# Two attention and feed-forward layers with a routed expert layer: experts that finish and scatter their own rows, one program for each engine, root steps in PSUM and a new order of the tail's steps

## The chip, the cores and the metric

The kernel runs on one core of one Trainium2 chip. The metric is the device time of one execution in microseconds (us), the median of several executions. The engines are TensorE (PE: matmuls, with PEld for its weight loads), VectorE (DVE), ScalarE (ACT), GpSimd (POOL) and SyncE (SP, which here only issues DMAs). A queue name such as SPq stands for an engine's sequencer that issues a DMA.

## The reference

Input x is 2048 tokens of 128 features. Four sub-layers follow each other, each as x = layernorm(x + f(x)):

1. causal attention with 16 heads of 64 (q, k, v, softmax, output projection);
2. a feed-forward layer of 512 hidden features with weights quantised to -1, 0, 1;
3. an attention with quantised weights and activations; for data whose attention weights all round to zero its output is the projection's bias alone, and a check at run time decides whether that holds;
4. an expert layer. Each token goes to the one of 16 experts with the highest score, and takes a place there if fewer than 128 tokens came before it:

```
score = softmax(xf @ Wg + bg); gate = max(score); idx = argmax(score)
pos   = running number of the token within its expert;  keep = pos < cap   # cap = 128
y     = relu(buf @ W1[e] + b1[e]) @ W2[e] + b2[e]       # buf: the kept rows, by expert and place
out   = where(keep, y[idx, pos] * gate, 0)
x     = layernorm(x + out)
```

A token that finds no place keeps its own row: its result is layernorm(x).

## The kernel before, in words

The kernel is written engine by engine, with semaphores between them, in three programs (`nc.Block`) that run one after the other: `attention`, `attention1_general` and `experts`. Every block ends on all engines before the next begins.

**attention.** The first attention is cut into 320 units (a head, a group of 512 queries, a pair of 128-key tiles). For a unit PE makes scores (L762 to L765), ACT two exponents of it (L1032, L1035), POOL the low half of the float (L1479, `prob_lo = prob - prob_hi`), and PE weighs the values (L788 to L792). At the end of a head and group DVE divides (`invert` L1206, `normalise` L1215, L1219).

From unit 288 on, the *tail* is mixed in: the steps of the other sub-layers for four groups of 512 tokens (g0 to g3). Each engine walks through step numbers i; at number i it does its part of unit i and then the tail steps that the tables `PE_AT`, `ACT_AT`, `DVE_AT`, `POOL_AT` and `ONCE_AT` put there. The numbers are no times, only the order within an engine. For a group the steps are: `project` (PE L826 to L829, 96 matmuls), `norm.0` (DVE: L1284, then `statistics`), the scaling on ACT (L1077), `turn` (PE L840), `x1t` in two halves (ACT L1052, DVE L1293), four `up` (PE L849 to L855, ACT L1061, DVE L1300), four `down` (PE L873, L874), `norm.1` with `third` (DVE: L1284, `statistics`, L1308, `statistics`), `second` (POOL L1486), `third` (ACT L1077), `turn3` (PE L890, ACT L1083), `gate` (PE L898, `choose` on DVE), `count` (PE L573, L576, `slots` on DVE) and `scatter` (POOL L596: four indirect DMAs that put the rows in `expert_rows` in DRAM). `turn.1` and `span` (PE L884, DVE L1319, L1320) and `check` (DVE L1346 to L1370) make the run-time decision of sub-layer 3.

`statistics` calls `one_over_deviation` (L523 to L529): two small operations, twice a reciprocal, a product and a step, then a reciprocal; all of its 128 x 4 operands are in SBUF. Until unit 319 has been weighed the tail has two PSUM banks (4 and 5) for PE's results; a fill waits until the one before it in its bank was given up, which for `project` and `down` is done by the first instruction of `norm` (L1284).

**attention1_general** holds the whole third sub-layer behind an `If` that is not taken for these inputs.

**experts.** SP waits for all scatters and loads the rows back (L1911). PE turns them (L1964); then for each of 16 experts `up` (PE L1974), relu (ACT L1949), `down` (PE L1983), the bias (DVE L2006) and an indirect DMA from POOL that scatters 128 results to `expert_out` in DRAM (L1934). When all 16 have landed, SP loads them back in token order (L1920), DVE multiplies by the gate and adds x (L2011), takes statistics (L2015, L2018, `one_over_deviation`), ACT and DVE scale (L1955, L2025) and SP stores (L1925). The exponent for the gate is ACT L1943.

Of the kernel before, what the change touches and what calls it, by code (L numbers as in the profile page):

```python
# [14 lines left out]
F32 = mybir.dt.float32  # L15
F16 = mybir.dt.float16
BF16 = mybir.dt.bfloat16
I32 = mybir.dt.int32
# [36 lines left out]
ROW = D + 1  # L55
YE = 4
# [179 lines left out]
class Fill:  # L236


    def __init__(self, bank, turn):
# [6 lines left out]
ACT_STAGES = (("norm", 0), ("turn", 0), ("up", 0), ("up", 1), ("up", 2), ("up", 3), ("third", 0), ("turn3", 0), ("turn", 1))  # L246
DVE_STAGES = (("norm", 0), ("turn_low", 0), ("up", 0), ("up", 1), ("up", 2), ("up", 3), ("norm", 1),
              ("gate", 0), ("count", 0), ("span", 0))
POOL_STAGES = (("second", 0), ("scatter", 0))
PE_AT = ((292, 294, 296, 298, 299, 301, 302, 303, 304, 304, 305, 305, 318, 318, 322, 353, 353), (297, 300, 301, 306, 308, 308, 310, 311, 312, 312, 313, 313, 323, 328, 330, 343, 355), (307, 314, 317, 319, 321, 322, 323, 324, 325, 325, 326, 328, 333, 339, 349, 343, 354), (328, 329, 329, 329, 335, 336, 336, 338, 336, 338, 341, 341, 372, 374, 384, 373, 379))  # L250
ACT_AT = ((298, 299, 300, 302, 303, 305, 313, 319, 351), (306, 307, 309, 310, 311, 312, 325, 328, 347), (321, 323, 325, 326, 329, 330, 332, 339, 352), (331, 332, 334, 337, 341, 344, 355, 366, 386))
DVE_AT = ((290, 297, 299, 300, 303, 304, 307, 317, 324, 353), (301, 307, 307, 308, 309, 310, 311, 330, 338, 356), (316, 317, 320, 323, 326, 326, 332, 342, 352, 364), (332, 333, 333, 334, 340, 340, 342, 376, 396, 379))
POOL_AT = ((313, 369), (332, 390), (368, 408), (386, 414))
ONCE_AT = (289, 288, 292, 290, 296, 298, 308, 320, 329, 333, 359, 360, 288, 396)
# [135 lines left out]
class Tail:  # L390


    def __init__(self, nc, m, kept):
# [25 lines left out]
        self.gate = keep("gate", [P, TILES])  # L419
# [8 lines left out]
        self.work = [keep(f"work{i}", [P, TILES]) for i in range(3)]  # L428
        self.root = keep("root", [P, 2, TILES])
# [7 lines left out]
        self.ex = at("ex", w + 8192, [P, TILES, EXPERTS])  # L437
        self.stats16 = at("stats16", w + 9216, [P, TILES, 6])
        self.mv16 = at("mv16", w + 9600, [P, TILES, 2])
        self.rstd16 = at("rstd16", w + 9728, [P, TILES])  # L440
        self.shift16 = at("shift16", w + 9792, [P, TILES])
# [34 lines left out]
        self.xet = at("xet", m.PROB + 8256, [P, EXPERTS * CAP])  # L476
        self.b1r = at("b1r", m.PROB + 16448, [EXPERTS, FF])
        self.h = [at(f"h{i}", m.PROB + 18496 + 2048 * i, [P, FT, CAP]) for i in range(2)]
        self.ye = [at(f"ye{i}", m.PROB + 22592 + 512 * i, [P, D]) for i in range(YE)]
        self.er = at("e_r", m.HIGH[1], [P, TILES, D])  # L480
        self.back = at("back", m.KQ, [P, TILES, D])
# [5 lines left out]
        self.rows_out = nc.dram_tensor("expert_out", (S, D), F32, kind="Internal").ap()  # L487

    def sems(self, sem):
# [17 lines left out]
        self.ext_ready, self.asked, self.expd = sem("ext_ready"), sem("asked"), sem("expd")  # L507
# [11 lines left out]
def one_over_deviation(dve, c, t, out, variance, n=4):  # L519

    half, s, q = (work[:, 0:n] for work in t.work)
    half_eps, bits = (t.root[:, k, 0:n] for k in range(2))
# [9 lines left out]
def statistics(dve, c, t, x, n, g, off_ready=None):  # L532

    s = slice(4 * g, 4 * g + 4)
    for k in range(4):
        c.mark(dve.bn_stats(t.stats[:, k, :], x[:, k, :]))
# [4 lines left out]
    one_over_deviation(dve, c, t, t.rstd[:, n, s], t.mv[:, n, s, 1])  # L541
    last = dve.scalar_tensor_tensor(t.off[:, n, s], t.mv[:, n, s, 0], -1.0, t.rstd[:, n, s], ALU.mult, ALU.mult)
# [50 lines left out]

def scatter(pool, t, k):
# [4 lines left out]

def clear_rows(queue, t):  # L600
# [3 lines left out]
    queue.dma_start(t.rows_out.rearrange("(e c) d -> c e d", c=P), wide[:, :, 0:D]).then_inc(t.filled, 16)  # L604


def attention(nc, m, t, ins, sem):
# [46 lines left out]
    with nc.Block() as block:  # L654

        @block.tensor
        def _(pe):
            def take(what):
                if what.turns > 0:
                    pe.wait_ge(free[what.buf], what.turns)  # L660
                if what.after is not None:
                    pe.wait_ge(ride_placed, what.after.ride + 1)
                return m.buf[what.buf]

            def turn_x(job):
                b = job.group
                pe.wait_ge(x_loaded[b], 16)
                if b > 1:
                    pe.wait_ge(xt_low, b - 1)
                for t in range(4):  # L670
                    last = pe.transpose(m.psum[:, 6 + b % 2, t * P:(t + 1) * P], m.x[b // 2][:, 4 * (b % 2) + t, :], m.ident[:])
                last.then_inc(x_turned, 1)

            def kq(job):
                out = take(job)
                if job.pair == 0:
                    pe.wait_ge(xt_low, job.group + 1)
                    pe.wait_ge(w_low, 1)
                elif job.pair == 1:
                    pe.wait_ge(w_low, 4)  # L680
                c = slice(job.group * 512, (job.group + 1) * 512)
                w = slice(job.pair * P, (job.pair + 1) * P)
                for k in range(2):
                    o = out[:, k * 512:(k + 1) * 512]
                    pe.matmul(o, m.w_hi[:, k, w], m.xt_hi[:, c], start=True, stop=False)
                    pe.matmul(o, m.w_hi[:, k, w], m.xt_lo[:, c], start=False, stop=False)
                    last = pe.matmul(o, m.w_lo[:, k, w], m.xt_hi[:, c], start=False, stop=True)  # L687
                last.then_inc(full[job.buf], 1)

            def values(job):  # L690
                out = take(job)
                if job.pair == 0:
                    pe.wait_ge(xt_low, 2 * job.group + 2)
                    pe.wait_ge(w_low, 2)
                w = slice(job.pair * P, (job.pair + 1) * P)
                for t in range(8):
                    tok = slice((8 * job.group + t) * P, (8 * job.group + t + 1) * P)
                    o = out[:, t * P:(t + 1) * P]
                    pe.matmul(o, m.xt_hi[:, tok], m.w_hi[:, 2, w], start=True, stop=False)
                    pe.matmul(o, m.xt_hi[:, tok], m.w_lo[:, 2, w], start=False, stop=False)  # L700
                    last = pe.matmul(o, m.xt_lo[:, tok], m.w_hi[:, 2, w], start=False, stop=True)
# [1364 lines left out]
```

## Time and profile before

| what | value |
|---|---|
| median of three runs | 926.57 us (924.73 to 926.93) |
| profiled execution, own time | 924.85 us |
| its span | 923.0 us |
| PE, DVE, ACT, POOL busy | 790.1, 614.6, 634.3, 641.9 us |
| mean granted TensorE clock | 0.937 |
| attention's last weighing ends | about 788.8 us |
| last scatter of rows issued by POOL | 852.1 us |
| experts' rows loaded from | 860.1 us |
| last `down` ends | about 898.5 us |

The span runs from the program's first instruction to its last. A clock of 1.00 is 2.4 GHz and 0.50 is 1.2 GHz. Starts of instructions are in us from the start of the span, durations in us or, where marked mean, in ns.

### The profile page before, as it was taken

The numbers are of one execution on the slowest core, as the hardware profiler recorded it, in microseconds if no ns is written. First come the engines' busy times: TensorE is split into PE (matmuls) and PEld (weight loads), VectorE is DVE, ScalarE is ACT, GpSimd is POOL, SyncE is SP. The second block draws the span as 40 slices with busy tenths as digits, with TensorE's granted clock in tenths as the row PEclk, the third lists the DMA queues.
The fourth block names the chain that finished last, engine by engine and source line by source line (L and its number), as shares of the span: only waits on it lengthen the run. The fifth ranks groups of instructions, "written<-read, shape, count | busy, mean of one in ns | idle before, by whom it ended". The sixth has DMA issues, their size and how long they took to land. (4 is left out here: it accounts for less than half of the span.)

```text
span 923.0 us, 25964 instructions
## 1 busy us (share of the span) xinstructions
PE 790.1 (86%) x10829; PEld 516.5 (56%) x10829; DVE 614.6 (67%) x1338; ACT 634.3 (69%) x855; POOL 641.9 (70%) x401
## 2 busy tenths in 40 slices
PE   6778999989999999999999999999989975774590
PEld 3344555556666656665666566666657644542590
DVE  5697777677766767667766667766674749858015
ACT  4356777878888788888888888888876753231351
POOL 5356767878888888798878888898886736116050
PEclk9799999999999999999999999999999977856695
DMA  5222136141214122312322141214320100700353
GB/s 164 59 47 48 30 87 131 31 99 25 48 27 90 25 48 65 64 25 53 71 42 42 37 99 24 48 39 91 98 31 19 14 2 1 224 30 21 82 180 93
DMA packets 91087, 56.59 MB, mean 61 GB/s; under 512 B 39876, under 2 KB 87368, under 8 KB 90838
## 3 DMA queue, kind: packets, MB, share of 16 engines
q1 hardware_dynamic: 89222, 51.87, 24.9%
q8 instruction: 87, 1.43, 0.7%
q0 software_dynamic: 1024, 1.45, 0.5%
q10 hardware_dynamic: 720, 1.57, 0.5%
q14 instruction: 34, 0.28, 0.1%
HBM read 16.51 MB, written 5.26 MB: 24 GB/s over the span
## 5 line engine op out<-in xcount | busy, mean ns | idle before, releaser
L1479 POOL TENSOR_TENSOR prob_lo<-prob,prob_hi 128x1024 f16<-128x1024 f32 (+1 forms) x320 | 583.2, 1842 | 165.2 <-ACT prob L1035 127.0
L1171 DVE TENSOR_REDUCE part_max<-psum 128x2 f32<-128x1024 f32 (+1 forms) x320 | 333.3, 1059 | 87.4 <-PE psum L717 66.5
L1032 ACT ACTIVATE prob_hi<-psum 128x1024 f16<-128x1024 f32 (+1 forms) x320 | 288.5, 902 | 135.4 <-PE psum L765 131.2
L1035 ACT ACTIVATE prob<-psum 128x1024 f32<-128x1024 f32 (+1 forms) x320 | 288.5, 902 | 0.0
L762 PE MATMUL psum<-high 128*128 128x512 f16 (+3 forms) x640 | 225.4, 352 | 29.4 <-DVE part_max L1171 11.2
L788 PE MATMUL psum<-v,prob_hi 128*128 128x65 f16 x2176 | 235.0, 194 | 0.3 <-issue 0.2
L790 PE MATMUL psum<-v,prob_hi 128*128 128x64 f16 x2176 | 233.1, 193 | 0.0
L792 PE MATMUL psum<-v,prob_lo 128*128 128x65 f16 x2176 | 233.1, 195 | 0.0
L788 PEld LDWEIGHTS psum<-v,prob_hi 128*128 128x128 f16 x2176 | 201.0, 98 | 36.6 <-issue 17.1
L765 PE MATMUL psum<-mixed 65*128 65x512 f16 (+3 forms) x640 | 221.4, 351 | 0.0
L790 PEld LDWEIGHTS psum<-v,prob_hi 128*128 128x128 f16 x2176 | 202.0, 98 | 14.4 <-issue 0.6
L792 PEld LDWEIGHTS psum<-v,prob_lo 128*128 128x128 f16 x2176 | 201.6, 97 | 0.0
L717 PE MATMUL psum<-kq 64*128 64x512 f16 (+3 forms) x640 | 113.7, 358 | 13.6 <-DVE part_max L1171 5.1
L762 PEld LDWEIGHTS psum<-high 128*128 128x128 f16 x640 | 62.9, 98 | 88.9 <-issue 21.3
L1153 DVE TENSOR_TENSOR kq<-psum,kq 128x1024 f16<-128x1024 f32 x32 | 39.2, 1225 | 67.2 <-ACT kq L1002 67.2
L765 PEld LDWEIGHTS psum<-mixed 65*128 65x128 f16 x640 | 62.5, 98 | 36.8 <-issue 1.1
L717 PEld LDWEIGHTS psum<-kq 64*128 64x128 f16 x640 | 30.9, 93 | 68.3 <-DVE part_max L1171 23.4
L764 PE MATMUL psum<-mask_ki,corner 128*128 128x128 bf16 x256 | 56.0, 219 | 0.0
L1219 DVE SCALAR_TENSOR_TENSOR turned<-psum,inv_sum,turned 128x64 f16<-128x64 f32 x224 | 48.1, 278 | 2.0
L1162 DVE TENSOR_TENSOR v<-psum,v 128x512 f16<-128x512 f32 x32 | 20.6, 686 | 36.9 <-ACT v L1014 36.9
L1486 POOL TENSOR_SCALAR x<-r,mv,rstd 128x128 f32<-128x128 f32 x16 | 12.5, 794 | 45.1 <-DVE x L1308 45.1
L1002 ACT ACTIVATE kq<-psum 128x1024 f16<-128x1024 f32 x32 | 33.0, 1031 | 11.7 <-PE psum L687 11.1
(213 smaller groups left out, 920.4 us busy)
## 6 DMA issues: line engine op xcount, KB each, us to landing
high<-kq SPq DMA_DIRECT2D x128, 128.0 KB
mixed<-kq SPq DMA_DIRECT2D x64, 128.0 KB
ew<-in_L_ffn_W SPq DMA_DIRECT2D x32, 256.0 KB, 5.1
expert_rows<-zero SPq DMA_DIRECT2D x1, 1032.0 KB, 8.3
xe<-expert_rows SPq DMA_DIRECT2D x4, 258.0 KB, 4.1
prob<-in_L_attn_x SPq DMA_DIRECT2D x4, 256.0 KB, 5.9
mixed<-shift SPq DMA_DIRECT2D x64, 1.0 KB
expert_out<-zero SPq DMA_DIRECT2D x1, 1024.0 KB, 11.1
```

What stands on the lines that cost most here:

```text
L717: last = pe.matmul(o, m.kq_hi[rows, 1, q], m.kq_hi[rows, 0, k], start=(n == 0), stop=(c < g), skip_group_check=True)
L762: pe.matmul(o, k_hh[:, keys], q_hl[:, queries], start=True, stop=False)
L764: pe.matmul(o[:, 0:P], m.identb, m.mask_ki[:], start=False, stop=False)
L765: last = pe.matmul(o, k_l1[:, keys], q_hm[:, queries], start=False, stop=True)
L788: pe.matmul(acc[:, r, 0:HD + 1], hi[:, c], v[:, j, HD:VW], start=(j == 0 and r == 0), stop=False, skip_group_check=True)
L790: pe.matmul(acc[:, r, 0:HD], hi[:, c], v[:, j, 0:HD], start=False, stop=False, skip_group_check=True)
L792: last = pe.matmul(acc[:, r, 0:HD + 1], lo[:, c], v[:, j, HD:VW], start=False, stop=end, skip_group_check=True)
L1032: act.activation(m.prob_hi[i % HI_RING][:, 0:u.width], src, ACT.Exp, scale=EXP_SCALE)
L1035: act.activation(m.prob[i % PROB_RING][:, 0:u.width], src, ACT.Exp, scale=EXP_SCALE)\
L1171: last = dve.tensor_reduce(m.part_max[:, g % 2, :, r, c:c + 1], src[:, :, col:col + width], AX, ALU.max)
L1219: last = dve.scalar_tensor_tensor(lo[:, r, :], acc[:, r, 0:HD], inv[:, r:r + 1], hi[:, r, :], ALU.mult, ALU.subtract)
L1479: pool.tensor_tensor(m.prob_lo[i % LOW_RING][:, c], m.prob[i % PROB_RING][:, c], m.prob_hi[i % HI_RING][:, c], ALU.subtract).then_inc(low, 1)
```

## The change

- Each row that is scattered to an expert carries, besides its token's number, the share `1 / sum(exp)` (`ROW` 130 instead of 129). ACT makes the exponents by group (`ex`), DVE the share (`share`), both as new tail steps ahead of the scatter.
- The experts' DVE program first makes layernorm(x3) of all 2048 rows and SP stores them to the output (1 MB). For each expert DVE then forms gate * b2 + x (`spread`), adds gate * y (`add`), takes statistics, ACT takes a square root (`Sqrt`), DVE divides, and POOL scatters the finished rows over the output. The buffers `ye` are 7 instead of 4. The gathering back, the passes over 16 tiles and the last store are gone.
- The three programs are one: SP fetches the experts' rows as soon as the scatters have landed; the decision of sub-layer 3 is waited for on a semaphore (`judged`), and each engine reads it for itself.
- In `statistics` the operands `half`, `s` and the reciprocal for the offset are in the PSUM bank of the sum, so that no step reads two SBUF operands. One reciprocal is added, and the bank is given up at the end of the statistics and not after L1284.
- All tables of the tail's order are new. Among other moves PE's `project` of g2 (307, 314, 317) is at 315 and 316; DVE's `gate` of g1 goes behind `norm.0` of g3, and `gate` of g2 ahead of g3's `up`; DVE's `spread` goes ahead of `norm.1` of g2; ACT's `third` of g2 goes ahead of `norm.0` of g3; POOL's `scatter` of g0 goes ahead of `second` of g2.
- `clear_rows` clears one DRAM tensor and not two.

```diff
-ROW = D + 1
-YE = 4
+ROW = D + 2
+YE = 7
...
-PE_AT = ((292, 294, 296, 298, 299, 301, 302, 303, 304, 304, 305, 305, 318, 318, 322, 353, 353), (297, 300, 301, 306, 308, 308, 310, 311, 312, 312, 313, 313, 323, 328, 330, 343, 355), (307, 314, 317, 319, 321, 322, 323, 324, 325, 325, 326, 328, 333, 339, 349, 343, 354), (328, 329, 329, 329, 335, 336, 336, 338, 336, 338, 341, 341, 372, 374, 384, 373, 379))
+PE_AT = ((292, 292, 293, 298, 299, 300, 303, 304, 305, 305, 305, 306, 318, 318, 321, 372, 380), (297, 299, 300, 306, 309, 310, 311, 312, 312, 313, 313, 314, 326, 336, 341, 346, 373), (315, 316, 316, 318, 319, 322, 323, 326, 325, 330, 331, 332, 337, 338, 371, 373, 391), (333, 333, 333, 337, 344, 345, 348, 350, 351, 356, 357, 367, 404, 405, 424, 384, 415))
+ACT_AT = ((299, 299, 299, 301, 305, 306, 317, 323, 383, 326), (307, 310, 310, 311, 312, 314, 324, 334, 385, 365), (324, 324, 324, 327, 327, 329, 331, 336, 387, 374), (334, 336, 340, 342, 359, 364, 389, 402, 412, 423))
+DVE_AT = ((291, 293, 294, 295, 295, 304, 305, 316, 317, 373, 323), (294, 306, 306, 306, 309, 314, 314, 340, 370, 392, 366), (314, 316, 316, 320, 320, 325, 329, 353, 383, 415, 383), (334, 340, 354, 355, 357, 366, 372, 408, 433, 423, 431))
+POOL_AT = ((308, 364), (317, 464), (416, 483), (435, 490))
...
-    c.step(dve.scalar_tensor_tensor(half, variance, 0.5, half_eps, ALU.mult, ALU.add))
+    c.step(dve.tensor_scalar(half, variance, 0.5, 0.5 * EPS, ALU.mult, ALU.add))
...
-    c.step(dve.reciprocal(out, s))
+    c.mark(dve.reciprocal(out, s))
...
+    half, root, over = place[:, 0:4], place[:, 16:20], place[:, 32:36]
...
+    one_over_deviation(dve, c, t, t.rstd[:, n, s], t.mv[:, n, s, 1], half, root, t.work[:])
+    c.step(dve.reciprocal(over, root))
+    last = dve.scalar_tensor_tensor(t.off[:, n, s], t.mv[:, n, s, 0], -1.0, over, ALU.mult, ALU.mult)
...
+        c.step(dve.tensor_tensor(t.r[g][:], bank(fill).rearrange("p (a n) -> p a n", n=D), x, ALU.add))
+        statistics(dve, c, t, t.r[g], n, g, bank(fill), None if n else t.off_ready)
+        if n == 0:
+            give_up(fill, g, 0)
...
+        pool.wait_ge(t.shared, g + 1)
...
+    def sync(sp):
+        sp.wait_ge(t.scattered, 16 * TILES)
+        fetch(sp, t)
+        sp.wait_ge(t.judged, 1)
+        taken = sp.value_load(t.bad[0:1, 0:1], min_val=0, max_val=1)
...
+    def gpsimd(pool):
+        pool.wait_ge(plain_stored, 16 * GROUPS)
+        for e in range(EXPERTS):
+            if e % 4 == 0:
+                pool.wait_ge(t.xe_in[e // 4], 16)
+            pool.wait_ge(y_ready, e + 1)
+            pool.indirect_dma_start(rows_out, bass.IndirectOffsetOnAxis(xe[:, e, D:D + 1].bitcast(U32), 0),
...
+    def scalar(act):
+        act.wait_ge(t.zeroed, 7)
+        act.activation(t.spare[:], t.eps[:], ACT.Sqrt)
+        act.wait_ge(plain_var, 1)
+        act.activation(t.std16[:], t.mv16[:, :, 1], ACT.Sqrt, bias=t.eps[:]).then_inc(plain_root, 1)
...
+        def root(e):
+            act.wait_ge(row_var, e + 1)
+            act.activation(t.std_e[:, e:e + 1], t.mv_e[:, e, 1:2], ACT.Sqrt, bias=t.eps[:]).then_inc(row_root, 1)
...
+            last.then_inc(up_done, 1)
+            if e > 1:
+                root(e - 2)
+        root(EXPERTS - 2)
+        root(EXPERTS - 1)
...
+        def spread(e):
...
+            c.step(dve.scalar_tensor_tensor(ye[e % YE][:], t.eb2[:, e, :], xe[:, e, D + 1:D + 2], xe[:, e, 0:D],
+                                            ALU.mult, ALU.add))
+
+        def add(e):
+            y = ye[e % YE][:]
+            dve.wait_ge(down_full, e + 1)
+            dve.scalar_tensor_tensor(y, m.psum[:, 6 + e % 2, 0:D], xe[:, e, D + 1:D + 2], y, ALU.mult, ALU.add)\
+                .then_inc(down_done, 1)
+            dve.wait_ge(down_done, e + 1)
+            c.step(dve.bn_stats(t.stats_e[:, e % 2, :], y))
+            dve.bn_aggr(t.mv_e[:, e, :], t.stats_e[:, e % 2, :]).then_inc(row_var, 1)
+
+        def normal_rows(e):
+            y = ye[e % YE][:]
+            dve.wait_ge(row_root, e + 1)
+            c.step(dve.reciprocal(t.rstd_e[:, e:e + 1], t.std_e[:, e:e + 1]))
+            dve.tensor_scalar(y, y, t.mv_e[:, e, 0:1], t.rstd_e[:, e:e + 1], ALU.subtract, ALU.mult).then_inc(y_ready, 1)
...
+        for e in range(EXPERTS):
+            if e < EXPERTS - 1:
+                spread(e + 1)
+            add(e)
+            if e > 0:
+                normal_rows(e - 1)
+        normal_rows(EXPERTS - 1)
```

## Rows read from the trace of the kernel before

**Rows 1.** Busy time by stretch: PE, PEld, DVE, ACT, POOL, clock, DMA share, GB/s.

```profile
736.00:747.00 11.00, 3.11 (x17) 0.82 (x13) 8.02 (x31) 1.86 (x3) 2.12 (x1) 0.73 0.00 0
...
770.00:781.00 11.00, 0.69 (x23) 0.57 (x19) 10.34 (x32) 0.53 (x2) 7.66 (x7) 0.73 0.00 0
781.00:789.00 8.00, 7.15 (x74) 6.46 (x74) 5.58 (x37) 4.00 (x10) 0.00 (x0) 0.51 0.01 3
...
814.00:828.00 14.00, 13.84 (x65) 7.93 (x64) 7.43 (x33) 3.47 (x6) 0.00 (x0) 0.50 0.01 1
```

**Rows 2.** Timeline of DVE at two places: start, us, instruction, idle before.

```profile
731.40 2.10 DVE L527 TENSOR_TENSOR work<-work 128x4 f32<-128x4 f32 x1
...
733.95 1.87 DVE L527 TENSOR_TENSOR work<-work 128x4 f32<-128x4 f32 x1
...
760.55 0.69 DVE L1284 TENSOR_TENSOR r<-psum,x 128x512 f32<-128x512 f32 x1 [3.54 <-PE psum L874]
```

**Rows 3.** Groups of DVE's instructions, 728 to 782 us: busy, mean ns, idle.

```profile
L527 DVE TENSOR_TENSOR work<-work 128x4 f32<-128x4 f32 x8 | 8.8, 1097 | 0.3
L528 DVE SCALAR_TENSOR_TENSOR work<-work 128x4 f32<-128x4 f32 x8 | 5.1, 636 | 0.3
L1308 DVE SCALAR_TENSOR_TENSOR x<-r,rstd,pb_b 128x128 f32<-128x128 f32 x8 | 4.7, 645 | 0.1
...
L542 DVE SCALAR_TENSOR_TENSOR off<-mv,rstd 128x4 f32<-128x4 f32 x4 | 2.1, 520 | 0.1
```

**Rows 4.** One of the same groups, 796 to 836 us.

```profile
L528 DVE SCALAR_TENSOR_TENSOR work<-work 128x4 f32<-128x4 f32 x10 | 1.6, 162 | 0.3
```

**Rows 5.** Timeline of POOL at its last units, and a PSUM-reading group of DVE.

```profile
763.42 11.11 POOL L1479 TENSOR_TENSOR prob_lo<-prob,prob_hi 128x1024 f16<-128x1024 f32 x6
...
L1219 DVE SCALAR_TENSOR_TENSOR turned<-psum,inv_sum,turned 128x64 f16<-128x64 f32 x224 | 48.1, 278 | 2.0
```

**Rows 6.** Timeline of PE: the two long waits of the attention.

```profile
743.56 0.58 PE L849 MATMUL psum<-onesb,bias 3*128 3x512 bf16 x1 [6.48 <-DVE x1t L1293]
...
781.16 1.09 PE L890 MATMUL psum<-ident,x 128*128 128x128 f32 x4 [10.47 <-DVE r L1284]
```

**Rows 7.** Timeline, 784 to 863 us: ACT, DVE, POOL and SP.

```profile
784.38 1.65 ACT L1077 ACTIVATE x<-r,off,rstd 128x128 f32<-128x128 f32 x4 [1.50 <-DVE off L542]
...
797.51 0.68 DVE L1284 TENSOR_TENSOR r<-psum,x 128x512 f32<-128x512 f32 x1
...
831.97 3.15 POOL L1486 TENSOR_SCALAR x<-r,mv,rstd 128x128 f32<-128x128 f32 x4 [19.99 <-DVE x L1308]
...
852.10 0.98 POOL L596 DMA_INDIRECT expert_rows<-x,slotu  x1 [0.30 <-issue]
...
860.10 2.85 SPq L1911 DMA_DIRECT2D xe<-expert_rows  x4
```

**Rows 8.** DMA of the rows' scatter, from issue to landing, 800 to 870 us.

```profile
DMA to landing us min/median/max: 2.1/2.4/4.5
```

**Rows 9.** Groups of the experts' stage, 870 to 897 us.

```profile
L1949 ACT ACTIVATE h<-psum,b 128x128 f32<-128x128 f32 x64 | 18.2, 368 | 10.2 <-PE psum L1974 10.2
...
L2006 DVE TENSOR_TENSOR ye<-psum,eb 128x128 f32<-128x128 f32 x14 | 4.1, 292 | 21.6 <-PE psum L1983 21.6
```

**Rows 10.** Timeline from the last `down` to the end.

```profile
898.54 0.29 DVE L2006 TENSOR_TENSOR ye<-psum,eb 128x128 f32<-128x128 f32 x1 [1.20 <-PE psum L1983]
899.61 0.97 POOL L1934 DMA_INDIRECT expert_out<-ye,xe  x1 [0.53 <-issue]
901.83 2.02 SPq L1920 DMA_DIRECT2D back<-expert_out  x4
...
906.00 0.87 DVE L2015 BATCH_NORM_STATS2 stats<-e_r 128x6 f32<-128x128 f32 x4
```

**Rows 11.** Timeline of ACT: its one table load, and its smallest exponent.

```profile
3.27 1.28 ACT L1124 ACT_TABLE_LOAD   x1 [3.27 <-issue]
...
850.77 0.21 ACT L1116 ACTIVATE small<-small 1x16 f32<-1x16 f32 x1 [11.05 <-DVE small L1360]
```

More of the change, by code:

```diff
@@ L255 @@
+ONCE_AT = (288, 289, 290, 289, 294, 296, 316, 322, 329, 326, 359, 379, 309, 434)
 WIDE = ()
@@ L427, in __init__ @@
         self.off = keep("off", [P, 3, TILES])
-        self.work = [keep(f"work{i}", [P, TILES]) for i in range(3)]
-        self.root = keep("root", [P, 2, TILES])
+        self.work = keep("work", [P, 4])
+        self.root = keep("root", [P, 4])
         self.x = at("x", m.XT, [P, TILES, D])
@@ L591, in slots, with exponents_of, share @@
     dve.tensor_copy(t.slotu[:, s], t.slot[:]).then_inc(t.slots_ready, 1)
+def exponents_of(act, t, g):
+    s = slice(4 * g, 4 * g + 4)
+    act.activation(t.ex[:, s, :], t.lm[:, s, :], ACT.Exp).then_inc(t.ex_ready, 1)
+def share(dve, c, t, g):
+    c.step(dve.tensor_reduce(t.total[:], t.ex[:, 4 * g:4 * g + 4, :], AX, ALU.add))
+    dve.reciprocal(t.x3[g][:, :, D + 1], t.total[:]).then_inc(t.shared, 1)
 def scatter(pool, t, k):
@@ new lines, in scale, with place_third @@
+        def scale(g, n):
+            act.wait_ge(t.off_ready, OFFS.index((g, n)) + 1)
+            for k in range(4):
+                j = 4 * g + k
+                x = t.x3[g][:, k, 0:D] if n else t.x1[g][:, k, :]
+                last = act.activation(x, x if n else t.r[g][:, k, :], ACT.Identity, scale=t.rstd[:, n, j:j + 1],
+                                      bias=t.off[:, n, j:j + 1])
+            last.then_inc(t.x3_ready[g] if n else t.x1_ready[g], 1)
+        def place_third(g):
+            fill = wait_full(act, "turn3", g)
+            act.activation(t.x3t[g][:], bank(fill), ACT.Copy).then_inc(t.tail_free[fill.bank], 1)
@@ new lines, in third @@
+        def third(g):
+            x = t.x3[g][:, :, 0:D]
+            dve.wait_ge(t.early, 16 * 3)
+            for k in range(4):
+                last = dve.scalar_tensor_tensor(x[:, k, :], t.r[g][:, k, :], t.rstd[:, 1, 4 * g + k:4 * g + k + 1],
+                                                t.pb_b[:], ALU.mult, ALU.add)
+                if k < 3:
+                    c.mark(last)
+            last.then_inc(t.mean_ready, 1)
+            c.wait()
+            dve.wait_ge(t.mean_ready, g + 1)
+            fill = FILLS["down", g, 0]
+            statistics(dve, c, t, x, 2, g, bank(fill), t.off_ready)
+            give_up(fill, g, 2)
@@ new lines, in spread_rows @@
+        def spread_rows():
+            dve.wait_ge(t.row_in, 16 * 13)
+            c.mark(dve.reciprocal(t.prm[:, 0:2, :], t.row[:, QA:QA + 2, :]))
+            c.step(dve.tensor_scalar(t.prm[:, 2:4, :], t.row[:, QZ:QZ + 2, :], ROUND, -ROUND, ALU.add, ALU.add))
+            for n, src in enumerate((t.row[:, BQ:BQ + 2, :], t.prm[:, 0:2, :], t.prm[:, 2:4, :], t.row[:, QA:QA + 2, :])):
+                dst = t.spread[:, n, :].rearrange("a (b h d) -> a b h d", b=2, d=H1)
+                c.mark(dve.tensor_copy(dst, src.unsqueeze(3).broadcast_to([1, 2, HEADS, H1])))
+            c.wait()
@@ new lines, in vector @@
+        dve.memset(m.mixed[0][HD:HD + 1, 1, :], 1.0).then_inc(ones, 1)
+        run(PLAN[-1])
+        for i in range(NU):
+            if i > 1 and UNITS[i - 2].last:
+                invert(UNITS[i - 2])
+            run(PLAN[2 * i])
+            if i + 2 < NU and UNITS[i + 2].rider is not None:
+                place_shift(UNITS[i + 2].rider)
+            run(PLAN[2 * i + 1])
+            if i > 1 and UNITS[i - 2].last:
+                normalise(UNITS[i - 2])
+            tail(i)
+        invert(UNITS[NU - 1])
@@ L1878, in _ @@
[L1878 to L1884 removed]
+                    pe.wait_ge(dve_done, d0 + 10)
+                    for k in range(TILES):
+                        last = pe.transpose(flat(4)[:, k * P:(k + 1) * P], e[:, k * P:(k + 1) * P], m.ident[:])
```

2344 lines of the change are left out of this document (1148 added, 1196 removed).

## The prediction

> **What bounds the kernel now.** I began with busy time by stretch, because the page's shares are averages. In most of the 788 us of attention PE is full, but it did 3.11 us of work in the 11 us from 736 and 0.69 us in the 11 us from 770, and ran at 1.2 GHz for the 8 us behind that [rows 1]. PE's timeline names who ended those two waits: DVE both times, after 6.48 and 10.47 us [rows 6]. So I read DVE's timeline there. Four-element-wide products that take 0.16 us elsewhere took 2.10 and 1.87 us [rows 2, 4]. Grouped over 54 us, the products average 1097 ns, the steps 636 and the offset 520, where a quiet stretch has 162 for such a step [rows 3, 4]. At that time POOL ran its prob_lo subtractions end to end, 1.85 us each, and DVE's operations with one input in PSUM keep 278 ns all through the attention [rows 5]. The reader is to see that only operations with both inputs in SBUF stretch, and to about the length of a POOL instruction.
>
> Behind the attention one chain of small steps runs to the scatter. POOL sets its last part: from 831.97 it does second (3.15 us), then twelve scatters back to back, the last issued at 852.10 [rows 7]. Then nothing works until SP's fetch at 860.10, though a scatter lands in 2.4 us [rows 7, 8]. In the experts PE is full: 27 us hold 15 experts' worth, 1.79 us each, while ACT's four relus and DVE's bias wait for it [rows 9]. The last bias is at 898.54, its scatter at 899.61, the load back at 901.83, and the passes and the store run to 923.0 [rows 10].
>
> **The change, part by part**, against the profiled execution (span 923.0, own time 924.85).
>
> *Root steps in PSUM.* The long waits removed are 8 x (1.097 - 0.162) for the products, 8 x (0.636 - 0.162) for the steps and 4 x (0.520 - 0.162) for the offset: 7.5 + 3.8 + 1.4 = 12.7 us [rows 3, 4]. Of these 3.6 us lie in the first place (2.10 + 1.87 - 2 x 0.162) [rows 2], the rest, 9.0, in the second, and both chains are the ones PE waits for [rows 6]. L1308 has two SBUF inputs and stays as slow as it is (645 ns). What PSUM costs a small operation no row shows directly; L1219 has it at 278 ns for 64 elements, a step without it takes 162 for 4 [rows 4, 5]. I take 0 and, as the upper bound, 0.1 us for each of eight steps. The added reciprocal is one more small step with its wait: 0.2 us a statistics call. The Trainium skill, "SBUF — State Buffer" (section on the two sides), says that a VectorE operation with two SBUF inputs and a GpSimd operation that reads SBUF exclude each other for the whole instruction; by that rule, which the trace agrees with, L1308 still waits, and no root step does.
>
> *The new order, up to the last unit.* In the first place I walked through both orders with the durations of the rows. Sums and project of g0 are earlier, so norm.1 of g0 begins some 1.4 us earlier; PE's up of g1 (now at step 309, was 308) is ready 5.0 us earlier (3.6 + 1.4) and still finds DVE busy, since norm.1 and third last 11 us. Project of g2 moved behind down of g1 takes 48 matmuls, about 2.9 us, off the way to down. So norm.1 of g1, at 760.55 [rows 2], begins at about 752.6: 7.9 us earlier. From there to the scaling of g2 at 784.38 [rows 7] are 23.8 us. Less 9.0 of waits, less 1.4 for the division of unit 311 that now comes before it, plus three reciprocals (0.6), that is 14.0. The bank is now held until the statistics end, 3.5 us more for a project and 8.7 for a down. PE needs 11 us for the units and project up to step 318, so here it waits 2 to 3 us in place of 10.47, and that is all of the holds that I find exposed. ACT, which now scales third of g1 first, starts g2's scaling 0.6 late. Gain so far: 7.9 + 9.8 - 0.6 = 17.1 us.
>
> *The order behind the attention.* g2's last up now waits in PSUM bank 7 for the division of unit 319, which DVE does behind count of g0: 1.6 us late. The gate of g1 no longer stands before norm.1 of g2 (797.51 [rows 7], 2.0 us of DVE, of which 1.6 counted). The row parameters' spread, 1.3 us, now does. Four statistics calls add 0.8, and PE's gate and turn before g3's up take about what gate of g2 gives back. Net a loss of 2.1. So POOL's second of g3, at 831.97, starts 15.0 us earlier. From there POOL is the bound as before, 20.1 us to the last issue; DVE's slots of g3, with share and a span more, are ready within 0.5 us of POOL's need for them.
>
> *One program.* SP fetches when the scatters have landed, 852.10 + 2.4 = 854.5 in old time, not at 860.10: 5.6 us gained [rows 7, 8]. What hides behind the fetch (3 us to the first rows): the check, 6.5 us of DVE, ends before the last scatter is issued; each engine's reading of the decision, unpriced in the trace, costs between 0 and the 5.6 us of the old gap. The pass over 16 tiles comes behind it on DVE: 16 statistics at 0.22 and 16 aggregates, 5 us [rows 10], on which ACT's first square root waits, and behind that the evacuation of the turned rows. PE turns all four batches first, which gives it just under 1 us to spare; I take 0, the bound is 4. The store of 1 MB comes after the fetch on SP and ahead of the first result's scatter, some 8 us later.
>
> *The experts.* A 128x128 operation of DVE takes 0.29 [rows 9]; per expert there are now spread 0.29, add 0.29, statistics 0.22, aggregate 0.1, reciprocal 0.18 and normalise 0.25: 1.5 us with waits, under PE's 1.79. ACT has 4 x 0.284 = 1.14 and a root of one column, 0.21 by the smallest exponent [rows 9, 11]: 1.4. Both hide behind PE; without that cover, the excess over 1.79 is paid 16 times.
>
> *The end.* From 898.54: add 0.3, statistics and aggregate 0.4, the root of expert 15 beside normalise of 14, then normalise of 15: its row is ready at 900.3. POOL takes expert 14 at about 900.5 and needs 0.97 + 0.30 for each, so 15 goes at 901.8 and lands 2.15 later, as the old one did (899.61 to 901.76) [rows 10]: 904.0. Against 923.0 that is 19.0 gained.
>
> Sum: 17.1 - 2.1 + 5.6 + 19.0 = 39.6 us. Span 883.4, own time 885.3; the three runs' median is 1.7 above the profiled execution, so 887.
>
> **The rivals.** (a) *The banks held longer bite.* Only two banks serve the tail under the attention, and five fills before unit 319 are held 3.5 or 8.7 us longer, 27.9 in all. If half of that is exposed on PE, 14 us of the first gain go: 901. For it: DVE serves these steps in order, behind norms of 4 and 9 us. Against it: the fills of a group follow some units apart. (b) *PE keeps its clock.* With shorter waits the 14 us at 1.2 GHz from 814 and the 8 us from 781 [rows 1] may run at 2.4: up to half of the 22 us less, 876. For it: in these rows the clock is low in and behind stretches in which PE idled. Against it: the chain of g3 still idles PE. (c) *DVE becomes the experts' bound.* At 2.1 us instead of 1.5 it costs 16 x 0.3 = 5, 892. For it: six dependent operations with semaphores. (d) *ACT loads its table anew for every root and back.* One load, 1.28 us, served Copy, Exp, Identity and Relu for the whole run [rows 11]; Sqrt is new. If each root takes two loads and each drains an activation of 0.3 us first, ACT needs 1.4 + 2 x 1.6 = 4.6 us an expert, 2.8 over PE, 45 us in all, and the kernel is slower: 932. It decides from 1.79 + 39.6 / 16 = 4.3 us on. Against it: Copy, Relu and Exp already share a load. The Trainium skill, "ScalarE: Activation LUTs" (table sets), puts Sqrt in a set other than Exp's but Relu and Copy in every set; by that, one more load, hidden. The same page prices a switch at 2.66 us; two of those an expert would give about 966, an estimate.
>
> **How the numbers follow.** Forecast as summed 0.50, (a) 0.22, (b) 0.13, (c) 0.10, (d) 0.05. The range 874 to 902 takes in (a) to (c) and, around the forecast, PSUM's upper bound (some 4 us), the decision's reading (4 us) and the fetch. Of the forecast's cases none is slower. About 0.3% is what a measurement of this kernel can tell from no change. Faster 0.94, same 0.01, slower 0.05.
>
> **What would show it.** After: L527, L528 and L542's successors under 0.25 us beside POOL's subtractions, L1308's still at 0.3 to 0.7; PE's longest waits near 5 and 3 us; the fetch 2 to 3 us behind the last scatter's issue; experts at 1.79 us each and one further table load; last `down` to the end 5.5 us. The forecast is wrong if PE waits for banks 4 and 5 before unit 319 (a), if an expert takes over 1.9 us (c, d), or if PE waits for ACT or DVE after the rows have landed.

## The result and the profile after

The changed kernel took 892.65 us (889.11 to 896.50, four runs) against 926.17 for the kernel before on the same chip: ratio 0.9641, interval 0.9597 to 0.9684, 3.6% faster. I had forecast 887, in a range of 874 to 902. The profiled execution is the fastest of the four: span 887.3, own time 889.11, so its gain is 35.7 us of the 39.6 that I had summed.

Busy time by stretch, the stretches that answer to [rows 1], with some others of the same table left out:

```profile
736.00:747.00 11.00, 8.32 (x82) 4.27 (x83) 3.59 (x13) 4.09 (x7) 6.62 (x6) 0.69 0.00 1
...
770.00:781.00 11.00, 10.62 (x86) 5.93 (x83) 6.60 (x30) 2.75 (x6) 0.00 (x0) 0.50 0.15 28
...
797.00:814.00 17.00, 15.65 (x94) 9.36 (x94) 9.84 (x52) 5.96 (x14) 0.00 (x0) 0.57 0.03 8
```

PE now has work in the two stretches in which it had next to none: 8.32 us of 11 where it had 3.11, 10.62 of 11 where it had 0.69. But the second runs at 1.2 GHz (0.50) in its whole length, and so does most of 797 to 814: the clock that was low behind the waits is low in other stretches now, in which PE works. The small steps of DVE, grouped over 700 to 800 us (the columns are busy time and mean ns of one), answer to [rows 3] and [rows 4]:

```profile
L528 DVE RECIPROCAL work<-psum 128x4 f32<-128x4 f32 x19 | 3.5, 182 | 0.6
L1334 DVE SCALAR_TENSOR_TENSOR x<-r,rstd,pb_b 128x128 f32<-128x128 f32 x12 | 3.4, 349 | 0.1
...
L530 DVE SCALAR_TENSOR_TENSOR psum<-psum,work 128x4 f32<-128x4 f32 x20 | 3.4, 170 | 0.7
L529 DVE TENSOR_TENSOR work<-work,psum 128x4 f32<-128x4 f32 x20 | 3.1, 157 | 0.7
```

157 to 182 ns each (the offset, L547, 158). What took 1097 and 636 in the mean is gone, and PSUM costs a small step nothing. L1334 is the old L1308, with two inputs in SBUF: 349 ns here, where I had said that it stays at 645. What PE waited for up to 822, with the total, the number of waits and the longest (its two long ones of before, in the attention, were 6.48 and 10.47 [rows 6], and a third of 10.05, for ACT's scaling, stood behind it at 811.88):

```profile
PE psum L870 <- DVE x1t L1319: 5.3, 3, 4.5
PE psum L919 <- ACT x3t L1103: 4.8, 1, 4.8
PE psum L861 <- POOL x L1516: 4.2, 1, 4.2
...
PE psum L919 <- DVEq L1313: 2.0, 1, 2.0
```

The longest is 4.8 us, and only the 2.0 us for DVEq, DVE's late release of a bank, belong to the holds. The third wait listed is new: PE turns the rows that POOL's second makes, and stands behind it. The two ends of the part that I had put figures on are ACT's scaling of g2, at 767.41 for 784.38 [rows 7] (17.0 us earlier; I had 17.1), and POOL's second of g3 with the last scatter's issue:

```profile
767.41 1.63 ACT L1097 ACTIVATE x<-r,off,rstd 128x128 f32<-128x128 f32 x4
...
818.33 3.12 POOL L1516 TENSOR_SCALAR x<-r,mv,rstd 128x128 f32<-128x128 f32 x4 [25.59 <-DVE x L1334]
...
837.92 0.97 POOL L613 DMA_INDIRECT expert_rows<-x,slotu  x1 [0.30 <-issue]
```

818.33 for 831.97 is 13.6 us (I had 15.0), and from there POOL needs 19.6 us, as before 20.1. Then the timeline from the end of the check to the first expert:

```profile
839.50 0.14 DVE L1398 TENSOR_SCALAR bad<-small 1x1 int32<-1x1 f32 x1
840.04 2.04 SPq L621 DMA_DIRECT2D xe<-expert_rows  x4
840.60 1.28 ACT L1989 ACT_TABLE_LOAD   x1 [2.15 <-issue]
...
844.38 3.19 DVE L2076 BATCH_NORM_STATS2 stats<-x 128x6 f32<-128x128 f32 x16 [4.73 <-issue]
...
845.58 3.65 PE L2019 MATMUL psum<-ident,xe 128*128 128x128 f32 x16 [13.17 <-issue]
...
849.65 2.05 PE L2029 MATMUL psum<-xet,ew 128*128 128x128 f32 x16 [0.42 <-ACT xet L1994]
```

The fetch is at 840.04, 20.1 us earlier than [rows 7] has it. But the first rows have landed by 843.1, and PE turns them only at 845.58. The flag itself is late as well: the check ends at 839.64, 1.7 us behind the last scatter's issue, where I had it ahead of it, and all engines but SP read it from 839.68 on. The chain of waits says who was the last there:

```profile
840.66 3.71 issue
844.38 3.20 DVE stats L2076 x16
...
848.80 0.31 ACT std L1991
849.11 1.95 ACT xet L1994 x4
```

"issue" for 3.71 us is DVE, idle behind the flag that it wrote itself at 839.50. The trace's record of branch instructions shows what it does there: all five engines load the flag in 0.47 to 0.55 us, and then PE's branch over the general path takes 4.48 us (840.54 to 845.02); DVE's own branch takes 0.07, but its first instruction behind it begins 3.7 us later. ACT's, over a short path, takes 0.05. From DVE the chain goes on through the pass over the plain rows, ACT's root at 848.80 and ACT's copies, to PE's first up at 849.65. Fetch to first up is 9.6 us; before it was 7.6.

The experts, from the first up to the end of the last down, take 30.3 us (30.8 before). The end, from PE's last down:

```profile
878.76 1.16 PE L2038 MATMUL psum<-ew,h 128*128 128x128 f32 x8 [0.34 <-ACT h L2005]
...
879.96 0.35 DVE L2063 SCALAR_TENSOR_TENSOR ye<-psum,xe,ye 128x128 f32<-128x128 f32 x1
...
880.85 0.97 POOL L1983 DMA_INDIRECT out_x<-ye,xe  x1 [0.85 <-DVE ye L2073]
...
882.12 0.97 POOL L1983 DMA_INDIRECT out_x<-ye,xe  x1 [0.30 <-issue]
883.40 0.97 POOL L1983 DMA_INDIRECT out_x<-ye,xe  x1 [0.30 <-issue]
```

PE ends at 879.92, the last scatter is issued at 883.40 and has landed by 885.5. Last down to the end is 7.4 us; before, it was 24.5 [rows 10]. Step by step the gain of 35.7 is: up to the fetch 20.1, fetch to first up -2.0, the experts 0.5, the end 17.1.

### The profile page after: what moved, and what is told of

The parts are those of the page before. It is cut to its first block, busy times and chain, and to the rows that moved or that the text cites. A ratio compares the mean times of both kernels' runs of the same rounds, so it can differ in the third digit from the quotient of the medians.

```text
span 887.3 us, 26048 instructions
## 1 busy us (share of the span) xinstructions
PE 788.5 (89%) x10829; PEld 512.2 (58%) x10829; DVE 616.7 (70%) x1418; ACT 635.9 (72%) x869; POOL 640.9 (72%) x401
## 4 chain that ended last, share of the span: by engine, by line
PE 60%; DVE 23%; ACT 10%; issue 5%; DMA 1%; POOL 0%; SPq 0%; POOLq 0%; DVEq 0%; ACTq 0%
PE psum L783 12%; PE psum L786 10%; DVE part_max L1193 9%; PE psum L738 7%; PE psum L809 6%; PE psum L813 5%; PE psum L811 5%; ACT prob_hi L1052 3%; DVE kq L1175 3%; ACT prob L1055 3%; ACT kq L1022 2%; DVE turned L1241 2%; PE psum L2038 1%; ACT v L1034 1%; PE psum L2029 1%
## 5 line engine op out<-in xcount | busy, mean ns | idle before, releaser
L1983 POOL DMA_INDIRECT out_x<-ye,xe x16 | 15.5, 970 | 30.0 <-DMA out_x<-e_r 19.2
```

## The experiments

All runs have their own runs of the kernel before beside them (924.9 to 926.5 us). The first four build the change up from the kernel before: the root steps alone, the order alone, both, and both with one program.

**Root steps in PSUM alone.**

```diff
-    half, s, q = (work[:, 0:n] for work in t.work)
+    half, root, over = place[:, 0:4], place[:, 16:20], place[:, 32:36]
...
-    dve.tensor_tensor(t.r[g][:], bank(fill)..., x, ALU.add).then_inc(t.tail_free[fill.bank], 1)
-    wait_free(dve, "down" if n else "project", g)
+    c.step(dve.tensor_tensor(t.r[g][:], bank(fill)..., x, ALU.add))
+    ...
+    give_up(fill, g, 0)
```

> The kernel before with the root steps' operands in PSUM alone (bank kept until the statistics end, the second reciprocal added), its order, its three blocks and its experts as they were. My theory: the stretched steps and products fall to some 0.17 us each, 3.6 us in the first place where PE waits and 9.0 in the second, less 0.8 for four reciprocals and at most 2 for the banks held: 914 to 916 us against 926.2. Rival, the banks held longer bite in this order: over 920, with PE waiting for a bank of the tail. Rival, the steps were short in the changed kernel only because another order keeps them away from POOL's subtractions: they stay at 0.6 to 1.1 us here and the time stays at 926.

It took 936.0 us (932.2 to 944.2), ratio 1.0115 [1.0071, 1.0158]: 10 us slower than before, where my theory had 11 faster. Its steps, in the same kind of view (690 to 800 us), and PE's waits up to 822:

```profile
L1314 DVE SCALAR_TENSOR_TENSOR x<-r,rstd,pb_b 128x128 f32<-128x128 f32 x8 | 10.4, 1362 | 0.1
...
L527 DVE SCALAR_TENSOR_TENSOR psum<-psum,work 128x4 f32<-128x4 f32 x14 | 2.4, 170 | 0.5
```

```profile
PE psum L892 <- DVEq L1293: 10.8, 1, 10.8
PE psum L820 <- DVEq L1293: 9.9, 2, 7.2
PE psum L851 <- DVEq L1293: 3.2, 1, 3.2
```

The steps are as short as in the changed kernel though POOL's subtractions stand beside them as before, so it is PSUM that shortens them, not the order. The old wait of 6.48 us has all but gone (0.6). L892's 10.8 stands in the place of the old wait of 10.47, and the 13.2 us for L820 and L851 are new. PE's timeline has them as three waits of 2.7, 3.2 and 7.2 us, each for a bank that DVE gives up at the end of its statistics. L892 too now waits for such a release (DVEq) and no longer for the sum (L1284), so part of it is a hold as well; a fifth wait of this kind, 4.9 us, comes behind 822, at 847.52. And L1314, the large product with two inputs in SBUF, takes 1362 ns where it took 645, 5.7 us more in all: with the small ones gone, this one meets POOL's subtractions.

**The new order alone**, as a diff the five tables of steps, without the entries for the exponents and the share.

> The kernel before with the new order of steps alone (the steps for the exponents and the share left out of it). My theory: 1.4 us from sums and project of g0, 2.9 from project of g2 behind down of g1, less 2.1 lost behind the attention: 922 to 925 us against 926.2, with root steps that still take 0.6 to 1.1 us beside POOL. Rival, the order is what brought the gain inside the attention: 912 or less.

926.6 us (twelve executions), ratio 1.0005 [0.9989, 1.0021]. The order alone gives nothing. The stretch that PSUM would have taken away now falls on other steps:

```profile
L542 DVE SCALAR_TENSOR_TENSOR off<-mv,rstd 128x4 f32<-128x4 f32 x7 | 7.1, 1020 | 0.2
L523 DVE SCALAR_TENSOR_TENSOR work<-mv,root 128x4 f32<-128x4 f32 x7 | 6.7, 958 | 0.2
```

The offset takes 1020 and the first step 958 ns in the mean, where the product took 1097 before. Moving DVE's work against POOL's changes which step is hit.

**Both.**

> The kernel before with both: root steps in PSUM and the new order; three blocks and the experts as they were. My theory: the gains add up to 15.0 us at POOL's second of g3, so 911 us (909 to 914). If the two overlap (each takes the same wait away) the sum is less than that of the two single runs; if the order only pays once the steps are short, it is more than it.

910.9 us, ratio 0.9856 [0.9825, 0.9888]: 15.4 us faster, as forecast (15.0), though one part alone costs 9.7 and the other gives nothing. The two don't add up: with the short steps the order takes the exposed holds away (one of 2.1 us is left up to 822), and without the short steps it is worth nothing.

**Both and one program for each engine**, with the experts' old end.

> As the run before, and in addition one program for each engine, with the fetch of the rows ahead of the decision; the experts still scatter to the internal tensor, load back, and divide and normalise at the end (no exponents or share ahead of the scatter). My theory: 5.6 us less than with three blocks, 905 to 906. Against the changed kernel it should be some 13 us slower: 17 to 19 for the end, less some 4 to 5 for the pass over the plain rows that the changed kernel has between fetch and first expert. Rival, the block boundaries were hidden behind the scatters' landing: no more than 2 us less than with three blocks.

907.3 us, ratio 0.9797 [0.9768, 0.9825]: 3.5 us less than with three blocks, in place of 5.6, though the two intervals touch. The changed kernel, which differs by the experts' new end and the exponents and shares ahead of the scatter, took 892.7, 14.7 us less (I expected some 13). Its timeline from the last scatter's issue to the first expert:

```profile
842.99 0.97 POOL L611 DMA_INDIRECT expert_rows<-x,slotu  x1 [0.30 <-issue]
...
845.11 2.03 SPq L619 DMA_DIRECT2D xe<-expert_rows  x4
...
850.28 3.64 PE L2012 MATMUL psum<-ident,xe 128*128 128x128 f32 x16 [12.34 <-issue]
...
853.72 2.45 PE L2022 MATMUL psum<-xet,ew 128*128 128x128 f32 x14
```

The fetch is 2.1 us behind the last issue; with three blocks it was 7.8 (838.27 and 846.10). That is 5.7 us, where I had 5.6. But fetch to first up takes 8.6 us where it took 7.1: PE's jump over the general path now lies behind the fetch. The branch records of the kernel before show it at its old place, 3.62 us of PE from 856.11, between two block ends, inside the 8 us ahead of the fetch. Nothing hid it there: PE is the last engine to reach the second block's end, at 859.79, and the fetch follows at 860.10. So more than half of the 5.6 us is this jump, and it was moved, not removed.

**The changed kernel again**, for its spread and as the level for the runs beside it.

> The changed kernel once more, as the level for the three runs beside it: 892.7 us, 889 to 897. The kernel before spread by only some 4 us over 17 executions. If the granted clock of an execution goes with its time here too, the spread is the throttle's; if not, it is a wait that falls now one way and now the other.

893.6 us, ratio 0.9668 [0.9628, 0.9708]. Three executions took 889.3 to 889.9 at a mean granted clock of 0.950 to 0.956, three 897.4 to 898.7 at 0.941 to 0.943.

**The root steps' operands in SBUF again**, all else as changed.

```diff
-    half, root, over = place[:, 0:4], place[:, 16:20], place[:, 32:36]
+    half, root, over = (t.scratch[:, k, :] for k in range(3))
```

> The changed kernel with the three operands of the root steps in SBUF again and all else as it is, the banks still kept until the statistics end. In the three kernels run so far the order without PSUM roots gave 926.6 us and with them 910.9, so I expect what they gave there, some 15.7 us: 908 us (904 to 911). Rival, the new order alone keeps the small steps away from POOL's subtractions: under 897.

918.3 us, ratio 0.9913 [0.9885, 0.9941]. So, with banks that are held this long anyway, the roots' place in PSUM is worth 24.7 us; the rival is out, and my 15.7 was too little. PE's waits say why:

```profile
PE psum L871 <- DVE x1t L1320: 10.9, 3, 10.1
...
PE psum L912 <- DVEq L1314: 3.9, 1, 3.9
PE psum L871 <- DVEq L1314: 3.8, 1, 3.8
PE psum L920 <- DVEq L1314: 3.2, 1, 3.2
PE psum L840 <- DVEq L1314: 2.8, 1, 2.8
```

13.7 us of waits for banks given up late (DVEq) and 10.9 for DVE's low part. Stretched steps inside a held bank stretch the hold too. My 15.7 was from kernels of which the one without PSUM roots held nothing.

One row of this run goes against the reading that only operations with two SBUF inputs stretch:

```profile
L526 DVE TENSOR_SCALAR scratch<-mv 128x4 f32<-128x4 f32 x7 | 7.0, 998 | 0.2
```

This step has one SBUF input and constants, and writes to SBUF; four of its seven took 1.46 to 1.68 us. With its result in PSUM, as in the changed kernel, it takes 166 ns. The reciprocals, with one SBUF input too, stay at 178 ns or less in the mean.

**Old order, PSUM for the banks of down only.**

> The kernel before, old order, with root steps in PSUM for the statistics that use the bank of down (norm.1 and third) and in SBUF for those of the project (norm.0), whose bank is given up behind the sum as before. With all of them in PSUM it took 936.0 us and TensorE waited 13.2 us for banks given up late, in three waits (2.7, 3.2 and 7.2). Theory: the two shorter waits are for banks of a project, the 7.2 for one of a down; so some 6 us less with this one, 930, and still over the kernel before. Rival: the banks of down do no harm and nearly all the loss is the projects': 920 to 924, faster than the kernel before.

928.0 us, ratio 1.0024 [1.0001, 1.0047], 8 us less than with all roots in PSUM. PE's waits:

```profile
PE psum L893 <- DVE r L1287: 7.6, 1, 7.6
PE psum L821 <- DVEq L1298: 7.5, 1, 7.5
```

The two shorter waits are gone and the one of 7.5 us stays, which is the one for the bank of down. In the place of L892's 10.8 us PE waits 7.6 us for the sum, so some 3 of those were a hold too. The large product takes 1407 ns here. So the old order fails by both holds, and it is not faster even without the projects'.

**Without the decision.** The flag is not read and the general path is not there; this part of the computation is left out.

> The changed kernel without the reading of the flag and without the general path that it guards (that part of the computation is left out; the inputs don't need it). In the changed kernel's trace the branch takes TensorE 4.48 us and DVE about as long, and TensorE turns its first rows 2.5 us after they have landed. Theory: that is exposed, and with it the later start of the pass over the plain rows, so 2.5 us faster than the changed kernel, with the first transposes right behind the first landing. Rival: the landing of the rows and the plain pass hide it, same time within 1 us.

Its median, 893.8 us, ratio 0.9639 [0.9606, 0.9673], is that of the changed kernel. But its profiled execution was 4 us late at the very first sum (701.2 for 697.3), in code that is the same in both, and 7.1 at second of g3. This is no effect of the edit: in a later profile of the changed kernel itself (`after_third`) the sum is at 700.6 and second of g3 at 824.8, 6.5 late, and in both of these profiles the clock is at 1.2 GHz from 694 to 697, where it is at 2.4 in the first. What lies behind the fetch can still be compared: PE turns rows 2.9 us behind it in place of 5.5, the first up comes 6.6 us behind it in place of 9.6, and fetch to end takes 43.9 us for 47.3. But here the clock rises 6.3 us behind the fetch, ahead of the first up, and in the changed kernel 9.2 us behind it. So not all of the 3.4 us need be the decision's. The whole does not show it, so the rival is refuted for the piece alone.

**The decision turned round.** Nothing is left out.

```diff
+        with pe.If(taken < 1):
+            rest[0](pe)                 # the experts' part, for every engine
         with pe.If(taken):
             enter(pe)
...
             leave(pe)
+            rest[0](pe)
-                for part in (first, general, last):
+                for part in (first, general):
```

> The changed kernel with the decision turned round: the case that the inputs take falls through into the experts, which stand inside it, and the general path (with the experts once more behind it) lies behind them and is jumped over at the very end. Nothing is left out. Theory: a branch that is not jumped costs TensorE some tenths of a microsecond in place of 4.48, so the gain of the run without the decision less about 0.5: 2 us faster than the changed kernel. Rival: the long time is that of the reading or of any branch, jumped or not, and nothing is gained; the jump at the end could also cost some 4 us on the last engine.

890.2 us, ratio 0.9636 [0.9599, 0.9674].

```profile
840.42 2.03 SPq L621 DMA_DIRECT2D xe<-expert_rows  x4
...
841.06 3.19 DVE L2091 BATCH_NORM_STATS2 stats<-x 128x6 f32<-128x128 f32 x16 [1.04 <-issue]
...
843.44 3.87 PE L2034 MATMUL psum<-ident,xe 128*128 128x128 f32 x16 [10.51 <-DMA xe<-expert_rows]
...
847.10 1.28 PE L2044 MATMUL psum<-xet,ew 128*128 128x128 f32 x5
```

PE's branch takes 0.09 us, DVE begins its pass 1.0 us behind the flag, not 4.7, and PE turns the rows as they land. The first up is 6.7 us behind the fetch, for 9.6. But fetch to end is 46.3 us, only 1.0 less than in the changed kernel. The experts take 31.4 us for 30.3 and the end 8.2 for 7.4. In both kernels the granted clock is 0.56 to 0.58 from 845 to 850 and 1.00 from there: the work that PE takes up earlier it does at 1.2 GHz. The 0.8 us at the end are not the jumps of PE and DVE, which are done by 883.0. The last scatter lands 3.1 us behind its issue, where it took 2.2, and GpSimd's closing drain takes 4.95 us for 4.63; why both are longer is open.

> The kernel whose branch falls through, a second time. Its trace gave 1.0 us less from fetch to end than the changed kernel's, its median 3.4 less, with executions that spread by 10 us. If the gain is the 1.0 us of the trace, the two medians here differ by less than their spread can tell; if they are again over 2 us apart, something ahead of the fetch gained too.

> The changed kernel a third time, as the level for the run beside it: 893 us, 889 to 899.

887.2 us, ratio 0.9585 [0.9559, 0.9612], beside 889.6, ratio 0.9620 [0.9597, 0.9643], for the changed kernel. The two intervals overlap. Fetch to end is 45.8 for 47.0. Over all executions the medians are 888.6 (12) and 891.5 (15). This is the best kernel that I have, by 1.0 to 1.2 us from fetch to end in the two pairs of traces and by 2 to 3 in medians of executions that spread by 10. The medians are again over 2 us apart. The code ahead of the fetch is the same in both, so what could have gained there is the clock: it was 0.950 to 0.962 in the six executions of this kernel and 0.942 to 0.956 in the five of the changed kernel beside them. No run separates the two.

The profiles of the changed kernel also say what its spread is. PE worked at 1.2 GHz for 59.5 us in the first, with a span of 887.3, and for 72.3 us in the third, with 894.5 (its busy time within the stretches of that clock). The 12.8 us more at half speed are 6.4 of the 7.2 us between them.

**The last rows' order**, on top of it.

```diff
         for e in range(EXPERTS):
+            if e == EXPERTS - 1:
+                root(e - 2)
             act.wait_ge(up_full, e + 1)
...
+            if e == EXPERTS - 2:
+                normal_rows(e - 1)
             add(e)
```

> The kernel whose branch falls through into the experts (its profiled span from the fetch to the end was 46.3 us, against 47.3 in the changed kernel), and in addition the last three rows' order: expert 13's root stands before the relus of 15 on ACT, and its normalising before the sum of expert 14 on DVE, so that GpSimd does not get three scatters in a row behind the last matmul. Theory: row 13 leaves 1.3 us earlier, the last relus start 0.3 to 0.6 late, so 0.7 to 1.0 us less from the last rows' matmuls to the end: 45.4 us from fetch to end, 889 us in all where the clock falls as it did in that run. Rival: the last relus' delay takes it all, 46.3.

890.5 us, ratio 0.9615 [0.9588, 0.9641], fetch to end 46.7 us: nothing gained.

```profile
881.53 1.16 PE L2055 MATMUL psum<-ew,h 128*128 128x128 f32 x8 [0.63 <-ACT h L2022]
...
882.23 0.29 ACT L2013 ACTIVATE std_e<-mv_e,eps 128x1 f32<-128x1 f32 x1 [0.75 <-DVE mv_e L2084]
882.72 0.35 DVE L2080 SCALAR_TENSOR_TENSOR ye<-psum,xe,ye 128x128 f32<-128x128 f32 x1 [0.53 <-PE psum L2055]
...
883.70 0.34 DVE L2090 TENSOR_SCALAR ye<-ye,mv_e,rstd_e 128x128 f32<-128x128 f32 x1
...
884.84 0.97 POOL L1998 DMA_INDIRECT out_x<-ye,xe  x1 [1.02 <-DVE ye L2090]
886.11 0.97 POOL L1998 DMA_INDIRECT out_x<-ye,xe  x1 [0.31 <-issue]
```

ACT's last relus start behind root 13, and PE's last down waits 0.63 for them, where it waited 0.34: that much the rival had. The other part I had overlooked. Root 14 is there by 882.52 while DVE is idle, but DVE's order has the sum and the statistics of row 15 first, so row 14 is ready only at 884.04 and the scatters of 14 and 15 still come back to back, the last one 3.42 us behind the last down's end, where it was 3.48. The two rows' order would have to be changed together; that was not tried.

## Why the prediction was right, and where its terms were not

*Root steps.* Right in mechanism and in size: the steps are 0.16 to 0.18 us, and the run with SBUF operands brings the waits back. PSUM itself cost 0, as I had taken. The failed sentence is that L1308 "stays as slow as it is (645 ns)"; my list of signs had allowed 0.3 to 0.7. In the changed kernel it takes 349, in the two with the old order and operands in PSUM 1362 and 1407. What stretches is whichever two-input SBUF operation lies beside POOL's subtractions, so its mean belongs to a schedule and not to the instruction. This is how the Trainium skill, "SBUF — State Buffer" (section on the two sides), puts it, and for two-input operations these traces agree. Too narrow was my "only operations with both inputs in SBUF stretch": a step with one SBUF input took 998 ns in the mean in the run with operands in SBUF.

*The order up to the last unit.* 17.0 us measured for 17.1, but not by the parts that I had. The large product of g0, before and after:

```profile
736.46 2.94 DVE L1308 SCALAR_TENSOR_TENSOR x<-r,rstd,pb_b 128x128 f32<-128x128 f32 x4
...
733.14 1.14 DVE L1334 SCALAR_TENSOR_TENSOR x<-r,rstd,pb_b 128x128 f32<-128x128 f32 x4
```

norm.1 of g0 begins at 728.97 for 728.74, 0.2 us later where I had it 1.4 earlier. PE's up of g1 is 4.9 us earlier all the same (I had 5.0), because this product gave 1.8 us that I had put at nothing. norm.1 of g1 begins at 754.02, 6.5 us earlier for 7.9, and from there to the scaling of g2 the gain is 10.4 us for 9.2. That the sum is right to 0.1 us is luck. I had found only "2 to 3 us" of the holds exposed, and it is 2.0. Rival (a) is nevertheless no idle one: in the old order the same holds cost at least 13.2 us and turn the gain into a loss. I had judged it on the new order, and rightly, but had split the 17.1 into "waits" and "order" as if each could be had alone. The order's own 1.4 and 2.9 us, less the 2.1 behind the attention, don't exist by themselves: alone it gave 0.

*Behind the attention.* A loss of 3.4 where I had 2.1 (13.6 for 15.0 at second of g3). No run tells which of its small terms was short. POOL's 20.1 us were 19.6.

*One program.* The fetch came as forecast, 5.9 us closer to the last issue for 5.6. The step that failed is "I take 0, the bound is 4" for what lies behind it: it cost 2.0 us. Two things together make them: DVE and PE stand 3.7 and 4.5 us in the jump, and the pass over the plain rows, which I had behind the check with PE's work to hide it, starts that much later. I had named the decision "between 0 and the 5.6 us of the old gap" and put it behind the check, where I took the landing to hide it. I also had the check end before the last scatter is issued, and it ended 1.7 us behind it. Had it ended with that issue, PE's jump would have been over at 843.3, about when the first rows landed; that is worked out from the trace, no run tried it. In the run without the decision the piece from fetch to end is 3.4 us shorter, part of it at a higher clock.

*The experts.* 1.79 us each, DVE and ACT under PE, one further table load (1.28 us at 840.60). Rivals (c) and (d) are out.

*The end.* 17.1 for 19.0. The last issue was right (3.5 us behind the last down for 3.3), the landing too (2.1). I had let the kernel end with the landing; the kernel before ends 0.4 us behind the landing of SP's store. The changed kernel, whose last transfers are GpSimd's own, ends 1.8 us behind. The trace's records show GpSimd's closing drain run for 4.6 us and end 1.5 us after SP has seen the last landing.

*The median.* 3.5 above the profiled execution for 1.7, because the changed kernel's executions spread by up to 10 us where those of before spread by 4 to 7. Rival (b): PE's work at 1.2 GHz did not shrink, it moved (770 to 781 now; 797 to 814 at 0.57). All time at 1.2 GHz fell from 117 to 86 us (mean clock 0.937 and 0.952), but PE worked for 56 us of it before and for 60 now, so no gain came from it.

Every large term was right within 2 us. Of the 3.9 us that the sum had too much in the profiled execution, 2.0 lie between the fetch and the first up and 1.9 at the end; 0.5 lost ahead of the fetch and 0.5 gained in the experts cancel.

## What to carry to other kernels

An operand moved into PSUM is free for the instruction and not for the bank: count how long each bank is held and who wants it next, and lay out the order for that, since here the same edit cost 10 us in the old order and gave 16 in the new one (926.6 to 910.9). Before taking a block boundary out, ask what lies inside it and where that goes: here a jump of 3.6 us over a large body moved from ahead of the fetch to behind it. Put the path that the data takes where it falls through; here that gave 1.0 to 1.2 us from fetch to end.

## What the runs showed that I had not expected

- PE's jump over the general path took 3.3 to 4.9 us in every kernel that has it (4.48 here, 3.62 before), ACT's and GpSimd's, over shorter paths, 0.04 to 0.05; not jumped, the same branch took PE 0.09. The length alone does not set it: in the kernel that falls through, PE jumps at the end over the general path and a second copy of the experts, also in 3.62 us.
- GpSimd's last indirect DMAs are followed by the program's end 1.6 to 1.8 us behind their landing; after SP's store it was 0.4.
- Removing the small operations from POOL's way lengthened the one left, from 645 to 1362 ns.
- The mean granted clock of an execution and its time go together in nearly all of these kernels: in the second run of the changed kernel 0.950 to 0.956 for 889.3 to 889.9 us and 0.941 to 0.943 for 897.4 to 898.7 (in the third 0.942 stands beside 892.7), which sets what a difference of 2 or 3 us in medians is worth.
